# Condition mixing and a quantised gated FFN on one core: new head, scale folded into the down weight, other order of the loop

## The chip, the cores and the metric

The kernel runs on one NeuronCore of a Trainium2 chip. Its engines are TensorE (PE in the profile, PEld for its weight loads), VectorE (DVE), ScalarE (ACT), GpSimd (POOL) and SyncE (SP, which only issues DMAs here). The metric is the device time of one execution in microseconds (us).

## The reference

`x` is (64, 32, 512) in f32: 64 batches of 32 channels by 512. Each batch is mixed over its channels with one of 16 matrices of 32x32, picked by an integer token, and each of the 2048 rows of the result then goes through a quantised gated FFN (512 to 256 to 512). The FFN's result is added to `x`.

```
y = einsum('bct,bcd->bdt', x, weights[token]).reshape(-1, 512).astype(bf16)
for m in (gate, up):                      # dynamic quantisation of each row
    xs = y * inv[m];  scale = max(max|xs| / 127, 1e-8);  q = clip(round(xs / scale), -127, 127)
    h[m] = (q @ w[m].T) * scale * s[m]    # w holds whole numbers up to 127
inter = clip(silu(h[gate]) * h[up], -10, 10).astype(bf16)
xm = inter * inv_inter;  scale_m = max(max|xm| / 127, 1e-8);  qm = clip(round(xm / scale_m), -127, 127)
out = x + (qm @ w_down.T) * scale_m * s_down
```

## The kernel before, in words

The 2048 rows are 16 tiles of 128 rows (four batches each), all of `x` stays in SBUF (`x_sb`). Every engine has its own instruction queue, written out by hand; queues meet only through counting semaphores, and each engine executes its queue in the order written. For a tile t the steps are, with engine and line:

- `mix_in_batch` (TensorE, L560): one f32 product of the block-diagonal 128x128 `mix_all[:, t]` with the 128x512 tile into `y_ps`.
- `y_out` (ScalarE, L255): `y_ps` to bf16 `y_bf`. `smooth` (GpSimd, L206): `xs` = `y_bf` times both smoothing vectors, 128x1024.
- `amax_in`, `scale_in` (VectorE, L359, L364, L367): row maxima of `xs`, the scale, its reciprocal.
- `quantise` (ScalarE, L262): two activations of 128x512 that scale and round (a large bias leaves the whole number in the low f16 bits). `transpose_q` (TensorE, L566): eight 128x128 transposes to `qt_ps`. `q_out` (ScalarE, L269): to bf16 `q_t`.
- `gate_up` (TensorE, L582): eight products, 256 columns each, to `gu_ps`. `gate_up_out` (VectorE, L373): times the weight scales, to `gu`. `gate_silu` (ScalarE, L274). `intermediate` (VectorE, L378), `clip` (VectorE, L385).
- `smooth_mid` (GpSimd, L215), `amax_mid` and `scale_mid` (VectorE, L390, L395, L398), `quantise_mid` (ScalarE, L281), `transpose_mid` (TensorE, L597), `qm_out` (ScalarE, L288).
- `down` (TensorE, L610): two products of 512 columns into `o_ps`. `down_out` (VectorE, L406): times row scale and `s_down`, to `ffn`. `residual` (GpSimd, L222): plus `x`, to `res`, which SyncE stores.

The stages of different tiles are interleaved: in turn i of the loops ScalarE does `qm_out(i-6)`, `quantise(i-2)`, `quantise_mid(i-5)`, `gate_silu(i-3)`, `y_out(i)`, `q_out(i-2)`, and TensorE `gate_up(i-3)`, `mix_in_batch(i)`, `transpose_q(i-2)`, `down(i-6)`, `transpose_mid(i-5)`.

In the head the weights are loaded as they are and transposed by TensorE (`weight`, L532), the vectors are loaded as broadcasts to 128 partitions, and `mix_all` is filled from two sources: for tiles 0 to 2 by one small DMA per batch, whose address comes from a token that `value_load` (L141, L245) reads into a register from `token_row` in SBUF; for tiles 3 to 15 at once, from rows that an indirect DMA gathered (`picked`), which go out to DRAM (`picked_dram`, L166) and come back as four strided DMAs (L173, semaphore `blocks_in`). The program tests a flag at its end, and would repeat all tiles with split weights if the weights were not exact in bf16; with these inputs it does not.

## Time and profile before

| | |
|---|---|
| three runs | 96.28, 96.28, 98.17 us (median 96.28) |
| span of the profiled execution | 96.0 us; its own total was not recorded, the median run is 0.3 us above the span |
| busy | PE 57.0 us (59%), PEld 36.1 (38%), DVE 72.1 (75%), ACT 62.9 (66%), POOL 67.5 (70%) |
| DMA | 12.05 MB, mean 126 GB/s |
| TensorE's granted clock | near full, but about half from 20 to 23.5 us and from about 86 us on |

Busy shares are means over three stages: a head until the first SiLU at 22.9 us, a loop of equal periods, and a tail from about 83 us, in which no new tiles enter.

### The profile page before, as it was taken

What the parts mean: (1) busy time and instruction counts of PE and PEld (TensorE: products, weight loads), DVE (VectorE), ACT (ScalarE), POOL (GpSimd) and SP (SyncE); (2) the same over time, 40 slices, a digit from 0 to 9 for tenths busy, and PEclk for the clock granted to TensorE, in tenths of its full rate; (3) what the DMA queues carried; (4) which work ended last, traced back from release to release, by engine and by line L of the source; (5) the groups of instructions that cost most, each with busy time, mean ns of one, the idle gap of its engine ahead of it and who ended that gap; (6) DMA issues with size and microseconds to landing.
All of it is one profiled execution on the core that took longest, in us unless ns stands there. A gap on an engine that the chain in (4) does not pass through costs nothing.

```text
span 96.0 us, 1583 instructions
## 1 busy us (share of the span) xinstructions
PE 57.0 (59%) x425; PEld 36.1 (38%) x430; DVE 72.1 (75%) x174; ACT 62.9 (66%) x113; POOL 67.5 (70%) x57
## 2 busy tenths in 40 slices
PE   0692737189559487595865958569594574305610
PEld 0691214164426344363443635436352353102100
DVE  5300059407798989999999999999999999996360
ACT  5000226813978999889898898988989878223100
POOL 5505094800858759999999999999999746925720
PEclk9999999966999999999999999999999999965555
DMA  1989639989412312063360633202202022020443
GB/s 33 230 291 376 180 106 272 251 153 321 136 43 73 111 22 92 38 181 117 112 219 6 213 111 111 109 7 109 91 18 109 3 109 106 7 109 0 180 149 114
DMA packets 8796, 12.05 MB, mean 126 GB/s; under 512 B 3026, under 2 KB 3922, under 8 KB 8786
## 3 DMA queue, kind: packets, MB, share of 16 engines
q1 hardware_dynamic: 7906, 10.08, 33.0%
q0 software_dynamic: 400, 1.31, 3.8%
q10 hardware_dynamic: 480, 0.54, 2.7%
q8 instruction: 4, 0.07, 0.3%
q14 instruction: 6, 0.05, 0.2%
HBM read 7.47 MB, written 4.46 MB: 124 GB/s over the span
## 4 chain that ended last, share of the span: by engine, by line
DVE 54%; issue 13%; DMA 11%; PE 11%; ACT 4%; POOL 2%; SPq 1%; POOLq 0%; ACTq 0%
DVE y_ps L359 13%; DVE ffn L406 12%; DVE gu L373 10%; DVE gu_ps L378 7%; DMA raw<-in_L_ffn_w_down 6%; PE gu_ps L582 5%; DMA picked<-in_L_cond_weights,tokens 5%; DVE amax_m L390 4%; PE o_ps L610 3%; ACT q_t L269 3%; DVE rscale L367 2%; PE y_ps L560 2%; POOL raw L195 1%; DVE rest L414 1%; DVE rest_sums L418 1%
## 5 line engine op out<-in xcount | busy, mean ns | idle before, releaser
L206 POOL TENSOR_TENSOR xs<-y_bf,inv_in 128x1024 f32<-128x1024 bf16 x15 | 32.1, 2142 | 10.2 <-ACT y_bf L255 9.6
L582 PE MATMUL gu_ps<-w_t,q_t 128*128 128x256 bf16 x128 | 17.6, 283 | 17.4 <-ACT q_t L269 17.4
L262 ACT ACTIVATE q<-xs,rscale 128x512 f32<-128x512 f32 x32 | 21.4, 724 | 2.1 <-DVE rscale L367 2.1
L222 POOL TENSOR_TENSOR res<-ffn,x_sb 128x512 f32<-128x512 f32 x15 | 19.1, 1271 | 2.7 <-DVE ffn L406 2.7
L359 DVE TENSOR_REDUCE y_ps<-xs 128x2 f32<-128x1024 f32 x16 | 19.5, 1217 | 1.1 <-POOL xs L204 1.1
L560 PE MATMUL y_ps<-x_sb,mix_all 128*128 128x512 f32 x32 | 17.3, 625 | 4.7 <-DMA mix_all<-in_L_cond_weights 2.5
L582 PEld LDWEIGHTS gu_ps<-w_t,q_t 128*128 128x128 bf16 x128 | 11.7, 101 | 21.4 <-ACT q_t L269 20.0
L269 ACT ACTIVATE q_t<-qt_ps 128x1024 bf16<-128x1024 f16 x16 | 16.2, 1014 | 0.3 <-PE qt_ps L566 0.3
L255 ACT ACTIVATE y_bf<-y_ps 128x512 bf16<-128x512 f32 x16 | 9.3, 581 | 10.1 <-PE y_ps L560 10.1
L373 DVE TENSOR_TENSOR gu<-gu_ps,s_in 128x512 f32<-128x512 f32 x16 | 10.9, 683 | 5.5 <-PE gu_ps L582 5.5
L215 POOL TENSOR_TENSOR xm<-clipped,inv_mid 128x256 f32<-128x256 bf16 x16 | 11.7, 732 | 3.6 <-DVE clipped L385 3.6
L406 DVE SCALAR_TENSOR_TENSOR ffn<-o_ps,scale_m,s_out 128x512 f32<-128x512 f32 x16 | 11.9, 743 | 2.8 <-PE o_ps L610 2.8
L274 ACT ACTIVATE gu_ps<-gu,scale 128x256 f32<-128x256 f32 x16 | 7.6, 478 | 9.5 <-DVE gu L373 9.5
L566 PEld LDWEIGHTS qt_ps<-ident_f,q 128*128 128x128 f16 x128 | 8.3, 98 | 9.7 <-ACT q L262 6.2
L610 PE MATMUL o_ps<-w_t,qm_t 128*128 128x512 bf16 x27 | 9.7, 430 | 3.3 <-DVE ffn L406 3.1
L566 PE MATMUL qt_ps<-ident_f,q 128*128 128x128 f16 x128 | 9.8, 219 | 1.1 <-ACT q L262 1.0
L288 ACT ACTIVATE qm_t<-qmt_ps 128x256 bf16<-128x256 f16 x16 | 6.1, 382 | 4.7 <-PE qmt_ps L597 4.7
L281 ACT ACTIVATE qm<-xm,rscale_m 128x256 f32<-128x256 f32 x16 | 8.1, 506 | 0.0
L378 DVE SCALAR_TENSOR_TENSOR gu_ps<-gu,scale,gu_ps 128x256 f32<-128x256 f32 x16 | 7.5, 470 | 0.0
L560 PEld LDWEIGHTS y_ps<-x_sb,mix_all 128*128 128x128 f32 x32 | 5.1, 199 | 6.0 <-issue 5.8
L385 DVE TENSOR_SCALAR clipped<-gu_ps 128x256 bf16<-128x256 f32 x16 | 6.8, 424 | 0.5
L353 DVE TENSOR_TENSOR xs<-y_bf,inv_in 128x512 f32<-128x512 bf16 x1 | 0.7, 693 | 8.6 <-ACT y_bf L255 8.6
(40 smaller groups left out, 54.1 us busy)
## 6 DMA issues: line engine op xcount, KB each, us to landing
x_sb<-in_x SPq DMA_DIRECT2D x16, 256.0 KB, 3.5
out<-res SPq DMA_DIRECT2D x16, 256.0 KB, 2.0
raw<-in_L_ffn_w_gate POOLq DMA_DIRECT2D x1, 512.0 KB
raw<-in_L_ffn_w_up POOLq DMA_DIRECT2D x1, 512.0 KB, 7.6
raw<-in_L_ffn_w_down SPq DMA_DIRECT2D x1, 512.0 KB, 5.6
inv_in<-in_L_ffn_inv_gate ACTq DMA_DIRECT2D x1, 256.0 KB, 4.2
inv_in<-in_L_ffn_inv_up ACTq DMA_DIRECT2D x1, 256.0 KB, 5.5
picked_dram<-picked SPq DMA_DIRECT2D x1, 256.0 KB, 3.2
```

The source lines that it names most:

```text
L206: nc.gpsimd.tensor_tensor(xs[t % 2][:, :, :], y_bf[t % 2][:, :].unsqueeze(1).to_broadcast([P, 2, T]), inv_in[:, :, :], ALU.mult).then_inc( ...
L222: nc.gpsimd.tensor_tensor(res[t % RES][:, :], ffn[t % 2][:, :], x_sb[:, t * T:(t + 1) * T], ALU.add).then_inc(res_done, 1)
L262: nc.scalar.activation(q[t % 2][:, m, :], xs[t % 2][:, m, :], ACT.Copy, bias=ROUND_TO_F16, scale=rscale[:, t, m:m + 1]).then_inc(q_done, 1)
L269: nc.scalar.activation(q_t[t % 2][:, :, :, :], qt_ps[t % 2][:, :, :, :], ACT.Copy, bias=-float(OFFSET)).then_inc(qt_out, 1)
L359: nc.vector.tensor_reduce(y_ps[t % 2][:, 0:2], xs[t % 2][:, :, :], AX.X, ALU.max, apply_absolute_value=True).then_inc(amax_done, 1)
L373: nc.vector.tensor_tensor(gu[t % 2][:, :, :], gu_ps[t % 2][:, :, :], s_in[:, :, :], ALU.mult).then_inc(gu_out, 1)
L378: nc.vector.scalar_tensor_tensor(gu_ps[t % 2][:, 1, :], gu[t % 2][:, 1, :], scale[:, t, 1:2], gu_ps[t % 2][:, 0, :], ALU.mult, ALU.mult).t ...
L406: nc.vector.scalar_tensor_tensor(ffn[t % 2][:, :], o_ps[:, :], scale_m[:, t:t + 1], s_out[:, :], ALU.mult, ALU.mult).then_inc(ffn_done, 1)
L560: nc.tensor.matmul(y_ps[t % 2][:, :], mix_all[:, t, :], x_sb[:, t * T:(t + 1) * T], start=True, stop=True).then_inc(y_done, 1)
L566: last = nc.tensor.transpose(qt_ps[p][:, m, c, :], f16_low(q[p][:, m, c * P:(c + 1) * P]), ident_f16[:, :])
L582: last = nc.tensor.matmul(gu_ps[p][:, m, :], q_t[p][:, m, c, :], w_t[j][:, m, c * I:(c + 1) * I], start=(j == 0 and c == 0), stop=(j == pa ...
L610: last = nc.tensor.matmul(o_ps[:, :], qm_t[p][:, c, :], w_t[j][:, 2, c * T:(c + 1) * T], start=(j == 0 and c == 0), stop=(j == parts - 1 a ...
```

## The change

The arithmetic of the result stays. The host hands the weights over already transposed in chunks, and all vectors as one row, which TensorE spreads over the partitions with a column of ones (`widen`); VectorE and ScalarE copy them out of PSUM. `value_load` now reads the tokens straight from the input in DRAM, and several stand together ahead of their DMAs. `s_down` is multiplied into `w_down` once (`fold_s_down`), which makes it inexact in bf16, so it is split in three bf16 parts (`next_part`) and `down` has six products in place of two. `down_out` adds `x` itself and writes `res`; `residual` is gone. `clip` moves to GpSimd. The scale of the middle of tile t is computed together with that of the input of tile t+3, in one column block of `scale` (`MID_LAG`). Tiles' buffers become three or four deep, the first and last tile go in halves, and the order in all loops is new. The gate and up weights are read in place, every second bf16 of the f32 words.

```diff
-    WARM_UP = 52
+    WARM_UP = 36
+    XS, YB, QB, GB, MB = 4, 3, 3, 3, 3
+    MID_LAG = 3
...
+            sp.dma_start(rows[:, :], vectors.unsqueeze(0)).then_inc(rows_in, 16)
             load(0)
-            load(1)
-            sp.wait_ge(row_in, 16)
-            sp.wait_ge(mix_zero, 1)
-            for t in range(2):
-                for j in range(PER // 2):
-                    early_block(t, j)
-            load(2)
-            for j in range(PER):
-                early_block(2, j)
+            for t in range(EARLY):
+                s = [sp.value_load(token.unsqueeze(0)[0:1, t * PER + j:t * PER + j + 1], min_val=0, max_val=S - 1)
+                     for j in range(PER if t == 2 else PER // 2)]
+                if t == 0:
+                    sp.wait_ge(mix_zero, 1)
+                for j in range(len(s)):
+                    early_block(t, j, s[j])
+                if t + 1 < EARLY:
+                    load(t + 1)
+            sp.dma_start(flat(raw_down), w_down).then_inc(w_down_in, 16)
+            load(3)
             sp.wait_ge(picked_in, 16)
-            load(3)
-            sp.dma_start(raw[0][:, 2, :].rearrange("p (b k) -> p b k", k=I),
-                         w_down.rearrange("(b p) k -> p b k", p=P)).then_inc(w_in[2], 16)
+            load(4)
...
+            def clip(t):
+                pool.wait_ge(inter_done, t + 1)
+                nc.gpsimd.tensor_scalar(clipped[t % MB][:, :], inter[t % MB][:, :], LIMIT, -LIMIT,
+                                        ALU.min, ALU.max).then_inc(clip_done, 1)
...
-            for i in range(TILES + 7):
-                if exists(i - 4):
-                    smooth_mid(i - 4)
-                if exists(i - 7) and i - 7 < TILES - 1:
-                    residual(i - 7)
-                if exists(i):
-                    smooth(i)
+            for t in range(4):
+                smooth(t)
+            for i in range(TILES):
+                clip(i)
+                smooth_mid(i)
+                if exists(i + 4):
+                    smooth(i + 4)
...
             for t in range(2):
-                for j in range(PER // 2, PER):
-                    early_block(t, j)
-            for i in range(TILES + 6):
-                if exists(i - 6):
-                    qm_out(i - 6)
+                s = [act.value_load(token.unsqueeze(0)[0:1, t * PER + j:t * PER + j + 1], min_val=0, max_val=S - 1)
+                     for j in range(PER // 2, PER)]
+                if t == 0:
+                    act.wait_ge(mix_zero, 1)
+                for j in range(PER // 2):
+                    early_block(t, PER // 2 + j, s[j])
...
+            y_out(0)
+            s_in_copy()
+            y_out(1)
+            y_out(2)
+            quantise(0)
+            y_out(3)
+            q_out(0)
+            quantise(1)
+            y_out(4)
+            for i in range(TILES + 2):
+                if exists(i):
+                    gate_silu(i)
                 if exists(i - 2):
-                    quantise(i - 2)
-                if exists(i - 5):
-                    quantise_mid(i - 5)
-                if exists(i - 3):
-                    gate_silu(i - 3)
-                if exists(i):
-                    y_out(i)
-                if exists(i - 2):
-                    q_out(i - 2)
+                    qm_out(i - 2)
+                if exists(i + 1):
+                    q_out(i + 1)
+                if exists(i + 2):
+                    quantise(i + 2)
+                if exists(i - 1):
+                    quantise_mid(i - 1)
+                if exists(i + 5):
+                    y_out(i + 5)
...
-            def scale_in(t):
-                dve.wait_ge(amax_done, t + 1)
-                nc.vector.tensor_scalar(scale[:, t, :], y_ps[t % 2][:, 0:2], 1.0 / QMAX, LEAST_SCALE,
+            def scale_columns(t, m, end):
+
+                if m < 2:
+                    dve.wait_ge(amax_done, halves_through(t) - (1 if split(t) and end == 1 else 0))
+                if end == 3:
+                    dve.wait_ge(amaxm_done, t - MID_LAG + 1)
+                nc.vector.tensor_scalar(scale[:, t, m:end], amax[:, t, m:end], 1.0 / QMAX, LEAST_SCALE,
                                         ALU.mult, ALU.max).then_inc(scale_done, 1)
-                dve.wait_ge(scale_done, t + 1)
-                nc.vector.reciprocal(rscale[:, t, :], scale[:, t, :]).then_inc(rscale_done, 1)
+                dve.wait_ge(scale_done, scales_through(t, end - 1))
+                nc.vector.reciprocal(rscale[:, t, m:end], scale[:, t, m:end]).then_inc(rscale_done, 1)
...
             def down_out(t):
                 dve.wait_ge(down_done, t + 1)
-                nc.vector.scalar_tensor_tensor(ffn[t % 2][:, :], o_ps[:, :], scale_m[:, t:t + 1], s_out[:, :],
-                                               ALU.mult, ALU.mult).then_inc(ffn_done, 1)
-
+                if t >= RES:
+                    dve.wait_ge(stored[t % RES], 16 * (t // RES))
+                nc.vector.scalar_tensor_tensor(res[t % RES][:, :], o_ps[:, :], scale[:, t + MID_LAG, 2:3],
+                                               x_sb[:, t * T:(t + 1) * T], ALU.mult, ALU.add).then_inc(res_done, 1)
...
+            def fold_s_down():
+                dve.wait_ge(w_down_in, 16)
+                dve.wait_ge(s_out_wide, 1)
+                nc.vector.tensor_tensor(w_out[0][:, :, :], raw_down[:, :, :],
+                                        o_ps[:, :].unsqueeze(1).to_broadcast([P, IC, T]), ALU.mult).then_inc(part_done, 1)
+
+            def next_part(j):
+                dve.wait_ge(part_done, j)
+                nc.vector.tensor_tensor(flat(w_out[j]), flat(w_out[j - 1]), bf16_top(flat(w_out[j - 1])),
+                                        ALU.subtract).then_inc(part_done, 1)
...
-            for i in range(2, TILES + 6):
-                if exists(i - 6):
-                    down_out(i - 6)
-                if exists(i - 2):
-                    gate_up_out(i - 2)
+            scales(1)
+            amax_in(2)
+            rest_in_gate_up()
+            fold_s_down()
+            for i in range(TILES + 1):
                 if exists(i):
-                    amax_in(i)
-                if i == 2:
-                    weight_out(2)
-                if exists(i - 3):
-                    amax_mid(i - 3)
+                    gate_up_out(i)
+                if exists(i - 1):
+                    amax_mid(i - 1)
+                if i == LAST - 3:
+                    smooth_gate(LAST)
+                if i == LAST - 2:
+                    amax_half(LAST, 1)
+                scales(i + 2)
                 if exists(i):
-                    scale_in(i)
-                if exists(i - 3):
-                    scale_mid(i - 3)
-                if exists(i - 2):
-                    intermediate(i - 2)
-                    clip(i - 2)
-                if i == TILES:
-                    rest_in_gate_up()
-                if i == TILES + 1:
-                    rest_in_down()
-                if i == TILES + 3:
+                    intermediate(i)
+                if i + 3 < LAST:
+                    amax_in(i + 3)
+                if i + 3 == LAST:
+                    amax_half(LAST, 0)
+                if i == 0:
                     raise_flag()
+                    next_part(1)
+                if i == 1:
+                    next_part(2)
+                if exists(i - 2) and i - 2 < LAST:
+                    down_out(i - 2)
+            for h in range(2):
+                down_out_half(h)
...
-
-            def down_products(p, parts):
-                for j in range(parts):
+                transposes_of_mid(t % MB, t % 2).then_inc(qmt_done, 1)
+
+            def down_products(a, dst, first, end):
+                for j in range(PARTS):
                     for c in range(IC):
-                        last = nc.tensor.matmul(o_ps[:, :], qm_t[p][:, c, :], w_t[j][:, 2, c * T:(c + 1) * T],
-                                                start=(j == 0 and c == 0), stop=(j == parts - 1 and c == IC - 1))
+                        last = nc.tensor.matmul(dst, qm_t[a][:, c, :],
+                                                bf16_top(w_out[j][:, c, first:end]),
+                                                start=(j == 0 and c == 0), stop=(j == PARTS - 1 and c == IC - 1))
...
-            mix_in_batch(0)
-            mix_in_batch(1)
-            weight(0)
-            mix_in_batch(2)
+            pe.wait_ge(ones_done, 1)
+            pe.wait_ge(rows_in, 16)
+            for t in range(4):
+                mix_in_batch(t)
             transpose_q(0)
-            weight(2)
-            for i in range(3, TILES + 6):
-                if exists(i - 3):
-                    gate_up(i - 3)
+            mix_in_batch(4)
+            for i in range(TILES + 2):
+                if exists(i - 2):
+                    transpose_mid(i - 2)
                 if exists(i):
-                    mix_in_batch(i)
+                    gate_up(i)
+                if i == 0:
+                    pe.wait_ge(ones_done, 2)
+                    pe.wait_ge(rest_done, 1)
+                    pe.wait_ge(part_done, 1)
+                    nc.tensor.matmul(flag_ps, ones_col[:, :], rest_sum[:, :], start=True, stop=True).then_inc(rest_total, 1)
+                if exists(i + 1):
+                    transpose_q(i + 1)
                 if exists(i - 2):
-                    transpose_q(i - 2)
-                if exists(i - 6):
-                    down(i - 6)
-                if exists(i - 5):
-                    transpose_mid(i - 5)
-                if i == TILES + 2:
-                    add_rests()
+                    down(i - 2)
+                if exists(i + 5):
+                    mix_in_batch(i + 5)
             pe.wait_ge(flag_done, 1)
             with pe.If(pe.value_load(flag[0:1, 0:1].bitcast(I32)) != 0):
```

**TensorE, one turn of the middle of the loop.** Names: `gu_ps` is written by `gate_up`, `y_ps` by `mix_in_batch`, `qt_ps` by `transpose_q`, `o_ps` by `down`, `qmt_ps` by `transpose_mid`. Before:

```order
L560 MATMUL y_ps<-x_sb,mix_all 128x512 [waits scale_done,x_in12]
L566 MATMUL qt_ps<-ident_f,q 128x128 [waits qt_out,q_done]
L566 MATMUL qt_ps<-ident_f,q 128x128 x7
L610 MATMUL o_ps<-w_t,qm_t 128x512 [waits ffn_done,qmt_out]
L610 MATMUL o_ps<-w_t,qm_t 128x512
L597 MATMUL qmt_ps<-ident_f,qm 128x128 [waits qmt_out,qm_done]
L597 MATMUL qmt_ps<-ident_f,qm 128x128
L582 MATMUL gu_ps<-w_t,q_t 128x256 [waits clip_done,qt_out]
L582 MATMUL gu_ps<-w_t,q_t 128x256 x7
```

Now:

```order
L647 MATMUL qmt_ps<-ident_f,qm 128x128 [waits qmt_out,qm_done]
L647 MATMUL qmt_ps<-ident_f,qm 128x128
L628 MATMUL gu_ps<-raw,q_t 128x256 [waits qt_out,inter_done]
L628 MATMUL gu_ps<-raw,q_t 128x256 x3
L628 MATMUL gu_ps<-raw,q_t 128x256 [waits qt_out]
L628 MATMUL gu_ps<-raw,q_t 128x256 x3
L610 MATMUL qt_ps<-ident_f,q 128x128 [waits q_done,qt_out]
L610 MATMUL qt_ps<-ident_f,q 128x128 x3
L610 MATMUL qt_ps<-ident_f,q 128x128 [waits q_done]
L610 MATMUL qt_ps<-ident_f,q 128x128 x3
L660 MATMUL o_ps<-w_out,qm_t 128x512 [waits res_done,qmt_out]
L660 MATMUL o_ps<-w_out,qm_t 128x512 x5
```

`transpose_mid` stands ahead of `gate_up` in both. Before, the order from one `gate_up` to the next was `mix_in_batch`, `transpose_q`, two products of `down`, `transpose_mid`; now it is `transpose_q`, six products of `down`, `mix_in_batch`, `transpose_mid`.

**ScalarE, one turn of the middle of the loop.** Before, from `qm_out` on:

```order
L288 ACTIVATE qm_t<-qmt_ps 128x256 [waits down_done,qmt_done]
L262 ACTIVATE q<-xs,rscale 128x512 [waits qt_done,rscale_done]
L262 ACTIVATE q<-xs,rscale 128x512
L281 ACTIVATE qm<-xm,rscale_m 128x256 [waits qmt_done,rscalem_done]
L274 ACTIVATE gu_ps<-gu,scale 128x256 [waits gu_out]
L255 ACTIVATE y_bf<-y_ps 128x512 [waits xs_done,y_done]
L269 ACTIVATE q_t<-qt_ps 128x1024 [waits gu_done,qt_done]
```

Now, from `gate_silu` on:

```order
L310 ACTIVATE gu_ps<-gu,scale 128x256 [waits gu_out]
L324 ACTIVATE qm_t<-qmt_ps 128x256 [waits qmt_done]
L305 ACTIVATE q_t<-qt_ps 128x1024 [waits qt_done,gu_done]
L292 ACTIVATE q<-xs,rscale 128x512 [waits qt_done,rscale_done]
L292 ACTIVATE q<-xs,rscale 128x512 [waits rscale_done]
L317 ACTIVATE qm<-xm,rscale 128x256 [waits qmt_done,rscale_done]
L285 ACTIVATE y_bf<-y_ps 128x512 [waits xs_done,y_done]
```

Before, `quantise_mid` (`qm`) was the last instruction ahead of the SiLU, and behind the SiLU stood `y_out` and `q_out`; now `qm` is the sixth instruction of the turn that the SiLU opens, and `q_out` the third.

**SyncE, start of the head.** Before:

```order
L152 DMA token_row<-in_itok_B_15 1x64
L138 DMA x_sb<-in_x 128x512 x2
L141 TENSOR_LOAD token_row [waits mix_zero,row_in]
L141 ISA x2
L142 ISA
L142 DMA mix_all<-in_L_cond_weights 32x32
L141 TENSOR_LOAD token_row
L141 ISA x2
```

Now:

```order
L185 DMA rows<-in_vectors 1x2304
L170 DMA x_sb<-in_x 128x512
L188 TENSOR_LOAD in_token_ptr
L188 TENSOR_LOAD in_token
L188 ISA x2
L188 TENSOR_LOAD in_token_ptr
L188 REGISTER_ALU
L188 TENSOR_LOAD in_token
L188 ISA x2
```

Each value takes two loads now, of the input's address (`in_token_ptr`) and of the token in DRAM, where it took one from SBUF; SyncE does this for eight tokens, all ahead of the DMA to `picked_dram`, and ScalarE for four.

## Rows read from the trace of the kernel before

**Rows 1.** The page's chain that ended last: share of the span by engine.

```profile
DVE 54%; issue 13%; DMA 11%; PE 11%; ACT 4%; POOL 2%; SPq 1%; POOLq 0%; ACTq 0%
```

**Rows 2.** Windows: stretch, length, busy us and instructions per engine, clock, DMA share, GB/s.

```profile
20.00:23.50 3.50, 3.50 (x16) 1.95 (x14) 1.31 (x2) 0.48 (x1) 0.00 (x0) 0.52 0.97 258
...
50.00:54.07 4.07, 2.90 (x23) 1.84 (x22) 3.97 (x11) 3.80 (x8) 4.01 (x5) 1.00 0.39 125
```

**Rows 3.** Timeline of ScalarE, one period: start, length, engine, line, operation.

```profile
52.66 0.38 ACT L288 ACTIVATE qm_t<-qmt_ps 128x256 bf16<-128x256 f16 x1
52.92 1.34 ACT L262 ACTIVATE q<-xs,rscale 128x512 f32<-128x512 f32 x2
54.15 0.51 ACT L281 ACTIVATE qm<-xm,rscale_m 128x256 f32<-128x256 f32 x1
54.93 0.48 ACT L274 ACTIVATE gu_ps<-gu,scale 128x256 f32<-128x256 f32 x1 [0.27 <-DVE gu L373]
55.34 0.58 ACT L255 ACTIVATE y_bf<-y_ps 128x512 bf16<-128x512 f32 x1
55.82 1.01 ACT L269 ACTIVATE q_t<-qt_ps 128x1024 bf16<-128x1024 f16 x1
56.73 0.38 ACT L288 ACTIVATE qm_t<-qmt_ps 128x256 bf16<-128x256 f16 x1
```

**Rows 4.** Timeline of an early period, GATE_UP products and SiLU.

```profile
25.24 1.05 PE L582 MATMUL gu_ps<-w_t,q_t 128*128 128x256 bf16 x8 [1.16 <-ACT q_t L269]
...
27.05 0.48 ACT L274 ACTIVATE gu_ps<-gu,scale 128x256 f32<-128x256 f32 x1 [0.64 <-DVE gu L373]
...
29.02 1.05 PE L582 MATMUL gu_ps<-w_t,q_t 128*128 128x256 bf16 x8 [1.42 <-ACT q_t L269]
```

**Rows 5.** Timeline of TensorE's matmuls, one period.

```profile
53.71 1.02 PE L560 MATMUL y_ps<-x_sb,mix_all 128*128 128x512 f32 x2
54.57 0.61 PE L566 MATMUL qt_ps<-ident_f,q 128*128 128x128 f16 x8
55.02 0.59 PE L610 MATMUL o_ps<-w_t,qm_t 128*128 128x512 bf16 x2
55.45 0.28 PE L597 MATMUL qmt_ps<-ident_f,qm 128*128 128x128 f16 x2
```

**Rows 6.** Waits: who waited for whom, us in total, times, longest.

```profile
ACT qm_t L288 <- PE qmt_ps L597: 4.7, 2, 3.5
```

**Rows 7.** SyncE's register loads of a token from SBUF, ns min/median/max.

```profile
L141 SPq TENSOR_LOAD <-token_row x8: 267/273/471, 2.1 to 10.5; - x8
```

**Rows 8.** VectorE's register load of the flag at the end, ns.

```profile
L506 DVEq TENSOR_LOAD <-flag x1: 833/833/833, 92.5 to 92.5; - x1
```

**Rows 9.** Timeline of SyncE's DMA issues in the head.

```profile
1.17 0.84 SPq L138 DMA_DIRECT2D x_sb<-in_x  x2
3.07 3.64 SPq L142 DMA_DIRECT2D mix_all<-in_L_cond_weights  x4
...
13.99 0.79 SPq L168 DMA_DIRECT2D raw<-in_L_ffn_w_down  x1
16.06 1.90 SPq L173 DMA_DIRECT2D mix_all<-picked_dram  x4
```

**Rows 10.** DMA issues by tensor: KB each, median us to landing.

```profile
picked_dram<-picked SPq DMA_DIRECT2D x1, 256.0 KB, 3.2
...
mix_all<-picked_dram SPq DMA_DIRECT2D x4, 52.0 KB, 3.2
```

**Rows 11.** Groups of instructions: busy us, mean ns, idle before.

```profile
L406 DVE SCALAR_TENSOR_TENSOR ffn<-o_ps,scale_m,s_out 128x512 f32<-128x512 f32 x16 | 11.9, 743 | 2.8 <-PE o_ps L610 2.8
L215 POOL TENSOR_TENSOR xm<-clipped,inv_mid 128x256 f32<-128x256 bf16 x16 | 11.7, 732 | 3.6 <-DVE clipped L385 3.6
...
L385 DVE TENSOR_SCALAR clipped<-gu_ps 128x256 bf16<-128x256 f32 x16 | 6.8, 424 | 0.5
```

**Rows 12.** Timeline of the last computation, VectorE.

```profile
92.47 0.69 DVE L503 TENSOR_TENSOR res<-ffn,x_sb 128x512 f32<-128x512 f32 x1
```

505 lines of the change are left out of this document (260 added, 245 removed).

## The prediction

> **What bounds the kernel now.** I read the chain that ended last first: VectorE has 54% of it, "issue" 13% [rows 1]. That is a mean over stages, so I looked at windows. In one period of 4.07 us in the middle VectorE is busy for 3.97, GpSimd for 4.01 and ScalarE for 3.80, TensorE for 2.90 at full clock [rows 2]: the loop is filled by VectorE and GpSimd together, and ScalarE is close behind. Then I read the timeline of one ScalarE period for what each activation takes when the next follows at once: from start to start SiLU 0.41, `qm_out` 0.26, `q_out` 0.91, the two of `quantise` 1.23, `y_out` 0.48, and `quantise_mid` lasts 0.51 [rows 3]. The reader is to see that only 0.27 us ahead of the SiLU is idle there: ScalarE alone could turn in about 3.7 us.
>
> Early on, while no `down` runs yet, the period is another: from `gate_up` at 25.24 to the next at 29.02, 3.78 us [rows 4]. It is a circle: `gate_up` to SiLU takes 27.05 - 25.24 = 1.81 us (products, then `gate_up_out`) [rows 4], then SiLU 0.41, `y_out` 0.48, `q_out` 1.01, and 0.05 for the semaphore [rows 3], sum 3.76. So a walk along the queues with these lengths gives the period to 0.02 us, and I use the same walk on the new order.
>
> **The change, the loop.** What it takes away is on the two full engines: `clip`, 0.42, and two small operations leave VectorE; `residual` leaves GpSimd, which gets `clip`. That one is not shown there: from below 0.42, VectorE's time for it, from above 0.73, the two-input `smooth_mid` of the same shape [rows 11]. I take 0.7, the row of the same engine. With GpSimd at 4.01 less a residual and plus 0.7, both engines have room for a period of 3.7. Merged scales, deeper buffers and the `x` added in `down_out` (0.74 as before, same shape [rows 11]) I cost at nothing: they lie on VectorE beside ScalarE's longer turn. If GpSimd's room were gone, the clip would cost its length in every turn.
>
> What the change adds is a new circle. Take the start of SiLU(i) as zero. ScalarE then does, in its order, SiLU 0.41, `qm_out` 0.26, `q_out` 0.91, `quantise` 1.23, `quantise_mid(i-1)` 0.51: that one ends at 3.32 [rows 3]. TensorE's next turn opens with `transpose_mid(i-1)`, which waits for it, and `gate_up(i+1)` stands behind that, though its own input was ready at 0.41 + 0.26 + 1.01 = 1.68. With 0.05 for the semaphore, 0.2 for the two transposes until the next product starts (between 0.1, if they only cost their columns, and their 0.28 [rows 5]) and 1.81 to SiLU(i+1), the period is 3.32 + 0.05 + 0.2 + 1.81 = **5.38 us**. Before, `quantise_mid` was the last activation ahead of the SiLU, and `transpose_mid` had no wait to show.
>
> There is a second circle on TensorE: `qm_out(i-2)` ends at 0.41 + 0.38 = 0.79, then come the six products of `down`, 3 times the 0.43 that two take from start to start, then the mix, 0.86 [rows 5]: 0.79 + 0.05 + 1.29 + 0.86 = 2.99. It ends ahead of 3.37, so the six products cost nothing as long as the first circle stands; without the first the period would be 2.99 + 0.2 + 1.81 = 5.0. Queued behind the waiting `transpose_mid` are `gate_up`, and through it `gate_up_out` on VectorE and the SiLU, so all engines idle.
>
> From SiLU(0) to SiLU(15): the first step has no `quantise_mid`, VectorE's turn with the flag and `next_part(1)` is the longest, about 4.0 (estimate from VectorE's operations, `next_part` at 1.2); the second lacks `qm_out`, 5.1; then 12 steps of 5.38 = 64.6; the last has no `quantise` left, 5.38 - 1.23 = 4.2. Sum **77.9**.
>
> **The head.** `mix_in_batch(3)` now stands ahead of `transpose_q(0)`, and it waits for `blocks_in`, the last link of a chain on SyncE. Per token, before: four blocks are issued in 3.64 us; with 0.42 for one issue (a pair of x loads takes 0.84) that is (3.64 - 0.42)/3 = 1.07 from one to the next [rows 9], of it 0.27 for the load from SBUF [rows 7]; 0.38 stays beside the issue. Now a token costs 0.38 + 2 L, L being one load, and eight of them stand in SyncE's queue ahead of `picked_dram`. L from DRAM is not shown: from below 0.27, the load from SBUF [rows 7]; the nearest from above is 0.83, the flag's load that has to wait for its engine [rows 8]; for the far end I go half as far again, 1.3. I take 0.55, the middle of the two rows, so 1.48 per token. SyncE: first two issues until 1.6 (a pair takes 0.84 from 1.17 [rows 9], one of them the new row of vectors), eight tokens 8 x 1.48 = 11.8, eight block DMAs 3.4, x loads 0.42 each for three, `w_down` 0.79 [rows 9]: `picked_dram` starts at 1.6 + 11.8 + 3.4 + 1.3 + 0.8 = 18.9. It lands 3.2 later; the last of four block DMAs starts 1.45 after the first (1.90 for all four [rows 9]) and lands 3.2 later [rows 10]. That is 26.8, and about 1 less since a megabyte of broadcasts is gone from the queues: **25.8**. Before, those four DMAs started at 16.06 [rows 9], now at about 22, so the head is 6 us later there.
>
> The Trainium skill has a floor for such a load (DMA: Bandwidth & Descriptors, "Latency and other measured facts": about 600 ns). By it L would be 0.6 and the sum 0.8 us longer; no row of this trace shows a load from DRAM.
>
> Behind `blocks_in`: TensorE has idled, and the row shows that it then runs at half clock for about 3.5 us (0.52 [rows 2]); mix(3) 1.7, transposes 0.9, mix(4) 1.7, then `gate_up` to SiLU(0) 1.8: **6.1**. The new second table load of ScalarE falls into ScalarE's wait there; if that cover were gone it would add its length, little over 1 us. Weights transposed by the host save TensorE 24 transposes that now lie beside the wait for DMA: nothing.
>
> **The tail.** From SiLU(15): SiLU 0.48 [rows 3], `intermediate`, clip, `smooth_mid` 0.5 + 0.7 + 0.73 [rows 11]. Then `down_out(13)` holds VectorE until about 3.0. `amax_mid` and scales 0.8, `quantise_mid` 0.51; `down(14)` in front until about 4.4; transposes, `qm_out` 0.38; `down` in halves, first 0.8, second 0.65 more, last half of `down_out` 0.45: 7.2. Behind the last computation, ending at 92.47 + 0.69 = 93.16 before [rows 12], come 2.8 us until the span's end. Sum **10.0**, against about 13 before.
>
> **Sum.** 25.8 + 6.1 + 77.9 + 10.0 = 119.8 us of span, against 96.0. The median of the runs is 0.3 above the span, so **120.1 us**, 25% slower.
>
> **Rivals.**
> - *Loads from DRAM cost no more than from SBUF*, L = 0.27 to 0.35, and landings of 2.5 in the lighter queues: `blocks_in` at 21 to 23, total 115 to 117. For it: both are loads into a register of the same sequencer. Against it: a way to DRAM and back. Chance 0.25.
> - *Loads from DRAM cost 1.3 or more*: 8 x 2 x 0.75 = 12 us more, 132. Chance 0.09.
> - *Faster*: the circle does not close, since TensorE takes the ready `gate_up` past the waiting `transpose_mid`. Then ScalarE's 3.7 bounds the loop. SiLU(0) at 32 (27 with cheap loads), 15 x 3.75 = 56, tail 10: 98.6, or 93.6 with cheap loads. It decides when the period is under 3.8 and the loads are cheap. Against it: in the tail ScalarE waited up to 3.5 us for `transpose_mid` [rows 6], whose `qm` was long written, since the queue held `down` in front, waiting for VectorE: matmuls stay in order. Chance 0.05. The same rival is that the change does only what its parts say.
> - *Strided weights at half rate*: `gate_up` and `down` now stream every second bf16. If that halves TensorE's rate, `gate_up` is 0.85 longer and the second circle binds (2.99 + 1.29 + 0.2 + 1.81 + 0.85 = 7.1): 145. No row shows a strided moving operand. Chance 0.03.
> - Between these (period near 5.0 or shorter, head early) 0.08, at 105 to 114.
>
> The forecast has 0.50. The range has to hold 8 in 10: from 111, the cheap loads with a period 0.3 shorter, to 129, loads of 0.83 (8 x 2 x 0.28 = 4.5) with periods 0.15 longer and a tail at half clock. A measurement of this kernel tells about 2% from no change. Faster by over 2%: 0.03; within 2%, 94.4 to 98.2: 0.03; slower by over 2%: 0.94.
>
> **What would show it.** Right: in the middle of the loop a period of 5.3 to 5.5 on all engines; the products of `gate_up` idle ahead, ended by the transposes or by `qm` of ScalarE; VectorE near 65% busy; ScalarE idle ahead of the SiLU for 1.6 us a turn; mix(3) late, at 26, behind blocks from `picked_dram`, with register loads of about 0.55 on SyncE; the first SiLU at 32. Wrong: a period under 4.5, `gate_up` starting 0.05 behind `q_out`, or mix(3) before 22.

## The result, and the profile after

The changed kernel takes **130.64 us** (median of four runs, 128.78 to 131.22); the kernel before, run beside it, 97.22 (median of four, 96.28 to 99.25). The ratio is 1.342, 95% interval 1.326 to 1.358: slower by a third. Some executions run one to five per cent longer than others of the same kernel, so each ratio here compares the faster executions only, and each time is the median of all. The forecast was 120.1, range 111 to 129: right in direction, with the top of the range 1.6 us too low. The profiled execution took 130.45 us, with a span of 128.7.

First the page's busy times and the chain that ended last, which answer [rows 1]:

```profile
PE 80.0 (62%) x463; PEld 43.8 (34%) x470; DVE 69.7 (54%) x140; ACT 66.0 (51%) x118; POOL 53.3 (41%) x55
...
PEclk9995555555589975699999999999999999999999
...
ACT 25%; PE 23%; issue 18%; SPq 15%; DVE 13%; DMA 3%; ACTq 0%; DVEq 0%
```

VectorE had 54% of the chain and now 13%; no engine is full. SyncE's queue, 1% before, has 15%, and it is all in the head. One window over a period, and one over the first turns of the loop (columns as in [rows 2]):

```profile
61.27:66.59 5.32, 3.80 (x25) 2.21 (x26) 3.63 (x8) 3.86 (x7) 3.19 (x3) 1.00 0.28 97
46.00:53.00 7.00, 5.23 (x24) 3.39 (x26) 4.38 (x9) 4.29 (x9) 5.88 (x5) 0.56 0.00 0
```

Every engine idles for at least 1.46 of 5.32 us, where two were full before. ScalarE's timeline shows what it waits for, one period, against [rows 3]:

```profile
61.27 0.48 ACT L310 ACTIVATE gu_ps<-gu,scale 128x256 f32<-128x256 f32 x1 [1.47 <-DVE gu L444]
61.69 0.36 ACT L324 ACTIVATE qm_t<-qmt_ps 128x256 bf16<-128x256 f16 x1
61.95 1.01 ACT L305 ACTIVATE q_t<-qt_ps 128x1024 bf16<-128x1024 f16 x1
62.85 1.33 ACT L292 ACTIVATE q<-xs,rscale 128x512 f32<-128x512 f32 x2
64.08 0.50 ACT L317 ACTIVATE qm<-xm,rscale 128x256 f32<-128x256 f32 x1
64.53 0.60 ACT L285 ACTIVATE y_bf<-y_ps 128x512 bf16<-128x512 f32 x1
66.59 0.48 ACT L310 ACTIVATE gu_ps<-gu,scale 128x256 f32<-128x256 f32 x1 [1.46 <-DVE gu L444]
```

TensorE in the same period, against [rows 5]:

```profile
62.34 1.30 PE L660 MATMUL o_ps<-w_out,qm_t 128*128 128x512 bf16 x5 [1.39 <-ACT qm_t L324]
63.48 1.02 PE L605 MATMUL y_ps<-x_sb,mix_all 128*128 128x512 f32 x2
64.63 0.29 PE L647 MATMUL qmt_ps<-ident_f,qm 128*128 128x128 f16 x2
64.75 1.07 PE L628 MATMUL gu_ps<-raw,q_t 128*128 128x256 bf16 x8
```

`qm` ends at 64.08 + 0.50 = 64.58, the transposes of `qmt_ps` start at 64.63, and `gate_up` follows at 64.75. Its own input `q_t` was there at 61.95 + 1.01 = 62.96. So for 1.8 us `gate_up` is ready and does not start. Most of that it stands behind `down` and the mix, which would let the next product start at 63.48 + 0.86 = 64.34 (the mix takes 0.86 from its start to the next product); the last 0.41 us are the wait of `transpose_mid` for `qm`. That 0.41 is what the first circle costs over the second, and experiment 5 gets it back.

In the head, SyncE's register loads (ns min/median/max), against [rows 7]. One token now needs one of each:

```profile
L188 SPq TENSOR_LOAD <-in_token_ptr x8: 828/842/1957, 1.6 to 19.0; - x8
L188 SPq TENSOR_LOAD <-in_token x8: 459/463/496, 3.3 to 19.9; - x8
```

SyncE's DMA issues from tile 2's blocks on, against [rows 9], and the landings of both transfers, against [rows 10]:

```profile
20.82 1.83 SPq L173 DMA_DIRECT2D mix_all<-in_mix_w  x4
22.69 0.42 SPq L196 DMA_DIRECT2D raw_down<-in_w_down  x1
23.16 0.43 SPq L170 DMA_DIRECT2D x_sb<-in_x  x1
23.64 0.53 SPq L199 DMA_DIRECT2D picked_dram<-picked  x1
24.21 0.56 SPq L170 DMA_DIRECT2D x_sb<-in_x  x1
28.37 2.13 SPq L204 DMA_DIRECT2D mix_all<-picked_dram  x4
```

```profile
picked_dram<-picked SPq DMA_DIRECT2D x1, 256.0 KB, 4.7
...
mix_all<-picked_dram SPq DMA_DIRECT2D x4, 52.0 KB, 2.1
```

What stands behind `blocks_in`: mix(3) on TensorE, then the second table load and SiLU(0) on ScalarE. The table load ends at 39.09 while `gu` was ready at 38.62, so it was not quite covered:

```profile
32.44 2.04 PE L605 MATMUL y_ps<-x_sb,mix_all 128*128 128x512 f32 x2 [6.50 <-issue]
...
37.81 1.28 ACT L310 ACT_TABLE_LOAD   x1
39.11 0.48 ACT L310 ACTIVATE gu_ps<-gu,scale 128x256 f32<-128x256 f32 x1
```

Later SiLUs start at 43.13, 49.23, 55.95 and 61.27, then every 5.32 us until 114.48, and the last at 118.64. The last computation answers [rows 12], and the clip on GpSimd [rows 11]:

```profile
125.94 0.48 DVE L471 SCALAR_TENSOR_TENSOR res<-y_ps,scale,x_sb 128x256 f32<-128x256 f32 x1 [0.20 <-PE y_ps L660]
...
L237 POOL TENSOR_SCALAR clipped<-inter 128x256 bf16<-128x256 bf16 x16 | 6.4, 399 | 38.8 <-DVE inter L451 38.8
```

### The profile page after: what moved, and what is told of

It reads as the page before. It is cut to its first block, busy times and chain, and to the rows that moved or that the text cites. A ratio compares the mean times of both kernels' runs of the same rounds, so it can differ in the third digit from the quotient of the medians.

```text
span 128.7 us, 1643 instructions
## 1 busy us (share of the span) xinstructions
PE 80.0 (62%) x463; PEld 43.8 (34%) x470; DVE 69.7 (54%) x140; ACT 66.0 (51%) x118; POOL 53.3 (41%) x55
## 3 DMA queue, kind: packets, MB, share of 16 engines
q10 hardware_dynamic: 480, 1.07, 2.6%
## 4 chain that ended last, share of the span: by engine, by line
ACT 25%; PE 23%; issue 18%; SPq 15%; DVE 13%; DMA 3%; ACTq 0%; DVEq 0%
ACT q L292 13%; SPq L188 11%; PE gu_ps L628 11%; DVE gu L444 8%; PE o_ps L660 6%; ACT qm_t L324 4%; ACT qm L317 4%; DMA x_sb<-in_x 3%; PE qmt_ps L647 3%; PE y_ps L605 3%; SPq L173 2%; ACT q_t L305 1%; DVE res L463 1%; SPq L170 1%; ACT L310 1%
## 5 line engine op out<-in xcount | busy, mean ns | idle before, releaser
L660 PE MATMUL o_ps<-w_out,qm_t 128*128 128x512 bf16 (+1 forms) x89 | 23.3, 395 | 19.5 <-ACT qm_t L324 17.8
L417 DVE TENSOR_REDUCE amax<-xs 128x2 f32<-128x1024 f32 x14 | 17.0, 1214 | 10.5 <-POOL xs L232 10.5
L237 POOL TENSOR_SCALAR clipped<-inter 128x256 bf16<-128x256 bf16 x16 | 6.4, 399 | 38.8 <-DVE inter L451 38.8
L628 PE MATMUL gu_ps<-raw,q_t 128*128 128x256 bf16 x128 | 17.9, 283 | 1.3 <-ACT q_t L305 1.3
L660 PEld LDWEIGHTS o_ps<-w_out,qm_t 128*128 128x128 bf16 x96 | 8.2, 99 | 29.2 <-ACT qm_t L324 19.7
L463 DVE SCALAR_TENSOR_TENSOR res<-o_ps,scale,x_sb 128x512 f32<-128x512 f32 x15 | 11.3, 750 | 6.8 <-PE o_ps L660 5.9
L605 PEld LDWEIGHTS y_ps<-x_sb,mix_all 128*128 128x128 f32 x32 | 6.8, 237 | 22.9 <-issue 21.5
L628 PEld LDWEIGHTS gu_ps<-raw,q_t 128*128 128x128 bf16 x128 | 11.9, 98 | 5.1 <-issue 3.1
L610 PE MATMUL qt_ps<-ident_f,q 128*128 128x128 f16 x128 | 10.7, 231 | 0.0
L647 PE MATMUL qmt_ps<-ident_f,qm 128*128 128x128 f16 x32 | 4.6, 224 | 7.5 <-ACT qm L317 6.4
L317 ACT ACTIVATE qm<-xm,rscale 128x256 f32<-128x256 f32 x16 | 8.0, 502 | 1.0 <-DVE rscale L429 1.0
L451 DVE SCALAR_TENSOR_TENSOR inter<-gu,scale,gu_ps 128x256 bf16<-128x256 f32 x16 | 7.5, 470 | 0.9 <-ACT gu_ps L310 0.7
```

The lines of the kernel that those rows point to most:

```text
L317: nc.scalar.activation(qm[t % MB][:, :], xm[t % MB][:, :], ACT.Copy, bias=ROUND_TO_F16, scale=rscale[:, t + MID_LAG, 2:3]).then_inc(qm_don ...
L417: nc.vector.tensor_reduce(amax[:, t, 0:2], xs[t % XS][:, :, :], AX.X, ALU.max, apply_absolute_value=True).then_inc(amax_done, 1)
L463: nc.vector.scalar_tensor_tensor(res[t % RES][:, :], o_ps[:, :], scale[:, t + MID_LAG, 2:3], x_sb[:, t * T:(t + 1) * T], ALU.mult, ALU.add ...
L605: nc.tensor.matmul(y_ps[t % 2][:, :], mix_all[:, t, :], x_sb[:, t * T:(t + 1) * T], start=True, stop=True).then_inc(y_done, 1)
L610: last = nc.tensor.transpose(dst[:, c, :], f16_low(q[a][:, m, c * P:(c + 1) * P]), ident_f16[:, :])
L628: last = nc.tensor.matmul(gu_ps[p][:, m, :], q_t[a][:, m, c, :], bf16_top(raw[j][:, m, c * I:(c + 1) * I]), start=(j == 0 and c == 0), sto ...
```

## The experiments

Theory A: two separate causes. Loads from DRAM in SyncE's queue hold the head up, and in the loop a circle through two in-order queues sets the period, no engine's work. The rivals were the six products of `down` (TensorE's work), the two engines VectorE and GpSimd, and TensorE's clock. For the ratios, the kernel before took 97.39 us beside experiments 1, 2, 5 and 6, 97.46 beside 7 to 10, 97.53 beside 4, 11, 12 and 13, and 96.95 beside 3, 14 and 15. Kernel 10 is the kernel of experiment 10, and so on; steps and periods are from one SiLU to the next.

**1. Tokens from SBUF in the changed kernel.**

```diff
+            sp.dma_start(token_row[:, :], token.unsqueeze(0)).then_inc(row_in, 16)
-                s = [sp.value_load(token.unsqueeze(0)[0:1, ...
+                s = [sp.value_load(token_row[0:1, ...
```

ScalarE's four loads are changed in the same way.

> The changed kernel with the tokens loaded once to SBUF (a 64-value row) and read into registers from there, as before the change; all else as in the change. Theory A (the register loads from DRAM hold SyncE back): a token costs about 0.7 us instead of 2.0, eight of them 10 us less, the product of tile 3 starts at about 22 to 23 us instead of 32.4, the loop keeps its period of 5.32, time 118 to 121. Rival B (the head is late by the DMAs' landings and their order, the loads are hidden beside them): less than 4 us gained, time 126 or more.

Measured: 118.67 us, ratio 1.223 (1.198 to 1.247), 12 us less than the changed kernel. SiLU(0) goes from 39.11 to 29.08, the period stays 5.32, and `picked_dram` is issued at 12.86, about where it stood in the kernel before (12.80):

```profile
12.86 0.57 SPq L203 DMA_DIRECT2D picked_dram<-picked  x1
```

So the loads are worth the 10 us before SiLU(0), and the loop does not care. About 2 of the 12 come later: the second and third step from SiLU to SiLU take 5.37 and 5.32 us here at full clock, and 6.10 and 6.72 in the changed kernel, partly at half clock.

**2. The reverse: tokens from DRAM in the kernel before.** The edit is the same in the other direction.

> The kernel before with one part of the change alone: the tokens are read into registers straight from DRAM. Theory A: eight tokens on SyncE cost 1.3 us more each, the product of tile 2 stands ahead of the second weight's transposes and tile 0's, so all behind it comes 9 to 10 us later: time 105 to 107, period 4.07 as before. Rival B: less than 3 us, time under 100.

Measured: 110.37 us, ratio 1.137 (1.116 to 1.159). SiLU(0) goes from 22.9 to 35.8, while the periods stay 4.07. It cost 3 to 5 us more than expected. The tokens' loads are those of the changed kernel, two for each, but both loads of the first token are much longer here, 2.40 and 2.19 us on SyncE (and 1.61 and 2.67 on ScalarE), which is most of the excess; why is open:

```profile
L141 SPq TENSOR_LOAD <-in_itok_B_ptr x8: 822/831/2402, 2.1 to 22.0; - x8
L141 SPq TENSOR_LOAD <-in_itok_B x8: 452/474/2193, 4.6 to 23.0; - x8
```

**3. Half of it: only tile 2's four tokens from SBUF**, the other eight from DRAM.

> The changed kernel with tile 2's four tokens read from SBUF and the other eight (four on SyncE, four on ScalarE) from DRAM as in it. Theory A (one price per token, 1.97 against about 0.65): 4 x 1.3 = 5.3 us off the time at which picked_dram is issued, less 0.4 for the added DMA, and so 4.5 to 5.5 us off the total: 125 to 126. Rival B (the first loads are dear and the later ones would be cheap anyway): 2 us or less. Rival C (the tokens of tiles 0 and 1, on ScalarE as well, hold the head by themselves, so that SyncE's later tokens hide): under 3 us.

Measured: 122.91 and 126.17 us, median 124.5, so 6.1 under the changed kernel; the profiled execution is the longer one. SiLU(0) goes from 39.11 to 33.66. `picked_dram` is issued at 18.31 instead of 23.64, 5.3 earlier for four tokens:

```profile
18.31 0.52 SPq L205 DMA_DIRECT2D picked_dram<-picked  x1
```

1.3 us per token, as theory A has it, net of the 0.4 for the added DMA. With two executions so far apart the total only excludes rivals B and C; the time of the issue is the sharper reading.

**4. The rest of the chain to `blocks_in`.** `picked_dram` ahead of `w_down` and x tile 3 on SyncE, the Silu table loaded at the start of ScalarE.

```diff
+            sp.wait_ge(picked_in, 16)
+            sp.dma_start(picked_dram, picked[:, :]).then_inc(picked_out, 16)
             sp.dma_start(flat(raw_down), w_down).then_inc(w_down_in, 16)
             load(3)
+            act.preload_act_table(ACT.Silu)
```

> The changed kernel, tokens from DRAM as in it, with picked_dram issued ahead of w_down and x tile 3 on SyncE, and the Silu table loaded at the start of ScalarE. Theory A (part of the 4.7 us landing of picked_dram, 3.2 before, is the 0.75 MB queued ahead of it, and the second table load holds SiLU(0) up by 0.4): picked_dram issued 0.9 earlier, landing 3.2, SiLU(0) 0.4 less: 2.5 to 2.8 us under the changed kernel. Rival B (4.7 is the DMA's own time, and the table load is hidden): 0.9 us or less.

Measured: 129.31 us, ratio 1.325 (1.309 to 1.342), 1.3 under the changed kernel and half of what theory A said:

```profile
picked_dram<-picked SPq DMA_DIRECT2D x1, 256.0 KB, 3.1
...
mix_all<-picked_dram SPq DMA_DIRECT2D x4, 52.0 KB, 3.8
```

The landing of `picked_dram` falls to 3.1, as expected, but the four block DMAs now take 3.8 instead of 2.1, probably because the 0.75 MB are still on their way then (no row names it). The wait moved from one link of the chain to the next. mix(3) starts 0.72 earlier and SiLU(0) 0.76: what is won is little more than the earlier issue. The table load is out of the way (SiLU(0) starts 0.04 behind `gu`, 0.48 in the changed kernel), but from mix(3) to `gu` it takes 0.42 longer, since full clock comes at the same time as before, 36.7 against 36.6, and so more of the stretch runs at half clock.

**5. `transpose_mid` behind what is ready.**

```diff
-                if exists(i - 2):
-                    transpose_mid(i - 2)
                 if exists(i):
                     gate_up(i)
                 if exists(i + 1):
                     transpose_q(i + 1)
                 if exists(i - 2):
+                    transpose_mid(i - 2)
                     down(i - 2)
```

> The changed kernel with one move on TensorE: the transposes of the middle stand behind gate_up and the transposes of q of their turn, ahead of down, and no longer ahead of gate_up. Theory A (a circle of SiLU, four activations, quantise_mid, transposes of the middle, gate_up): the circle opens, and the next one binds: SiLU 0.41, qm_out 0.38, 0.05, six products 1.29, mix 0.86, gate_up to SiLU 1.81, a period of 4.8, about 0.5 less in each of 13 turns, time 123 to 125. Rival C (the loop is held by TensorE's own work, or by ScalarE's): the period stays at 5.3, time 130.

Measured: 121.76 us, ratio 1.254 (1.227 to 1.282), 8.9 less. The period is 4.90 while mixes run, 0.42 less, and 4.04 in the last four turns, which have no mix; the expectation had left these out, and so asked for 1 to 3 us too little. TensorE in one period:

```profile
60.70 1.53 PE L660 MATMUL o_ps<-w_out,qm_t 128*128 128x512 bf16 x6 [1.04 <-ACT qm_t L324]
62.07 1.02 PE L605 MATMUL y_ps<-x_sb,mix_all 128*128 128x512 f32 x2
62.93 1.07 PE L628 MATMUL gu_ps<-raw,q_t 128*128 128x256 bf16 x8
```

That is the second circle of the prediction: `qm_out`, six products, mix, `gate_up` without a gap, and TensorE idle 1.04 ahead of `down`. Opening one circle gives only the distance to the next.

**6. Two products of `down` instead of six, in the changed order.** The two smaller parts of `w_out` are left out of the sum.

```diff
-                for j in range(PARTS):
+                for j in range(1):
...
```

> The changed kernel with two products in down instead of six; it leaves out the second and third part of the split down weight, so its output is less exact. Theory A: the products are hidden, since the transposes of the middle wait for ScalarE until 3.37 us behind the SiLU and the products and the mix are over at 3.0: the period stays at 5.3, a little gained in the first turns and the tail, time 127 to 129.5. Rival C (TensorE's added work is the cost): 0.86 less a turn, period 4.5, time 117 to 119.

Measured: 130.96 us (129.72 and 132.19): no gain from two thirds of `down` gone. The period stays 5.32 to 0.01 us, so TensorE's work is not the bound. The profiled execution, the longer one, went to half clock at 100.9 us, and three periods grew to 5.9 to 6.2, 2.4 us in all. That blurs the comparison of totals (127 to 129.5 were expected) but not that of the periods:

```profile
60.00:70.00 10.00, 6.03 (x43) 3.58 (x44) 6.53 (x14) 7.48 (x14) 6.36 (x6) 1.00 0.28 87
98.00:110.00 12.00, 7.22 (x40) 4.29 (x40) 7.05 (x14) 6.48 (x13) 3.27 (x5) 0.62 0.12 46
```

TensorE was granted 2.4 GHz in the first stretch and mostly 1.2 GHz in the second. In the 30 us before the clock fell it was busy for 16.7; in the same 30 us of the changed kernel, which kept 2.4 GHz, for 21.7.

**7. Both single repairs, 1 and 5.**

> The changed kernel with both single repairs at once: tokens read from SBUF, and transpose_mid behind gate_up and transpose_q on TensorE. Theory A (two separate causes, a queue of loads in the head and a circle in the loop, that add): SiLU(0) at 29, as with the tokens alone; periods 4.9 with a mix and 4.04 without, as with the order alone; SiLU(15) about 100 and total 111 to 112. Rival B (one gives back part of the other, through the clock of TensorE or through a shared wait): the two gains of 12.0 and 8.9 us do not add, total 114 or more.

Measured: 109.74 us, ratio 1.129 (1.115 to 1.144). SiLU(0) 29.14, periods 4.90 and 4.04. The gains of 12.0 and 8.9 add up to the 20.9 that is measured, so head and loop are separate. The total is 1.3 under the range expected.

**8. The loop opened wholly** (with tokens from SBUF, and with `down_out` one turn later on VectorE).

```diff
-            for i in range(TILES + 2):
-                if exists(i - 2):
-                    transpose_mid(i - 2)
+            for i in range(TILES + 3):
...
-                    down(i - 2)
+                    transpose_mid(i - 2)
+                if i <= TILES and exists(i - 3):
+                    down(i - 3)
```

> Tokens from SBUF, and the loop's order on TensorE opened wholly: gate_up(i), transpose_q(i+1), transpose_mid(i-2), down(i-3), mix(i+5), so that nothing on TensorE waits for what ScalarE does in the same turn; down_out goes one turn later on VectorE. Theory A (the period was a wait in an in-order queue, no engine's work): the period becomes the longest sum of one engine: TensorE 1.07 + 0.43 + 0.2 + 1.29 + 0.86 = 3.85, ScalarE 3.75, VectorE about 3.6; so 3.8 to 3.9, and the total 29 + 4 + 14 x 3.87 + 10.3 + 1.8 = about 99 to 101. Rival B (clip on GpSimd and the larger VectorE operations lengthen each other once they run side by side all the time, smooth 3.12 for 2.14): period 4.3 or more, total 106 or more.

Measured: 103.01 us, ratio 1.056 (1.037 to 1.076). The period is 3.98: theory A's side, but above its 3.87. The expected total was 99 to 101. The first four steps took 4.0, 4.9, 3.8 and 5.2 us, 2.3 more in all than the expectation had for them.

**9. The head in another order** besides: `picked_dram` ahead of tile 2's tokens, the weights' DMAs ahead of the copies, mix(3) behind `transpose_q(0)`, VectorE's weight work in turns 0 and 2, and smaller moves that the expectation lists.

> As the one before, and the head in another order: picked_dram is issued ahead of the third tile's tokens, weights ahead of inv_gate_copy, Silu table loaded at the start, mix(0) and mix(1) ahead of the widening of s_in and s_down, mix(3) behind transpose_q(0) and mix(4) behind gate_up(0), the pass over the low bits of the weights behind intermediate(0), the parts of w_out in turn 2. Theory A (what is left over before is the head's order, 29.1 against 22.9 to the first SiLU): SiLU(0) at 21 to 23, the loop 2 us longer for VectorE's extra work in turns 0 to 2, total 93 to 96, that is, just under before. Rival B (the head's length is TensorE at half clock whatever the order): SiLU(0) at 26 or later, total 98 or more.

Measured: 101.46 us, ratio 1.051 (1.035 to 1.067). SiLU(0) came at 24.4, between the two theories, and the total is on the side of rival B, for a reason that neither had: the third SiLU-to-SiLU step took 8.2 us. The two `next_part` passes together took 4.30 us beside GpSimd's `smooth`, against 2 x 1.28 in the changed kernel; `gate_up_out(3)` stood behind them on VectorE, and `down(0)` waited for them on TensorE (3.96 us). The head's gain was given back there.

**10. Four products of `down`** (third part of `w_out` left out).

> As the one before, with four products of down instead of six (the third part of w_out is left out, so s_down times w_down keeps 16 bits of its mantissa). Theory A (with the circle open, TensorE's own sum of 3.85 bounds the loop, and the six products count now, where in the changed kernel they were free): period 3.75, ScalarE's sum, and one pass of VectorE less in turn 2; 2 to 3.5 us under the one before. Rival B (another engine bounds the period already): no more than 1.3 us under it.

Measured: 97.54 us, ratio 1.004 (0.999 to 1.009). 3.9 us less, more than rival B allowed, but the period is still 3.97, so TensorE did not bound it; what was saved is the one pass in turn 2 (the third and fourth step took 5.1 and 4.4 us instead of 8.2 and 5.1). VectorE's timeline of one period shows the bound, and the last row is the GpSimd operation that runs beside:

```profile
57.59 0.68 DVE L451 TENSOR_TENSOR gu<-gu_ps,s_in 128x512 f32<-128x512 f32 x1
58.18 0.41 DVE L463 TENSOR_REDUCE amax<-xm 128x1 f32<-128x256 f32 x1
58.70 0.56 DVE L433 TENSOR_SCALAR scale<-amax 128x3 f32<-128x3 f32 x1
59.30 0.18 DVE L436 RECIPROCAL rscale<-scale 128x3 f32<-128x3 f32 x1
59.39 0.47 DVE L458 SCALAR_TENSOR_TENSOR inter<-gu,scale,gu_ps 128x256 bf16<-128x256 f32 x1
59.77 1.21 DVE L424 TENSOR_REDUCE amax<-xs 128x2 f32<-128x1024 f32 x1
60.90 0.74 DVE L470 SCALAR_TENSOR_TENSOR res<-o_ps,scale,x_sb 128x512 f32<-128x512 f32 x1
61.56 0.68 DVE L451 TENSOR_TENSOR gu<-gu_ps,s_in 128x512 f32<-128x512 f32 x1
...
57.09 2.14 POOL L236 TENSOR_TENSOR xs<-y_bf,inv_in 128x1024 f32<-128x1024 bf16 x1
```

Hardly a gap on VectorE, and 0.56 us for a scale of three numbers per row. It ends at 59.26, `smooth` at 57.09 + 2.14 = 59.23.

**11. `intermediate(i)` ahead of `scales(i+2)`** on VectorE, nothing else.

> The version with four products, with one edit: on VectorE intermediate(i) stands ahead of scales(i+2). Theory A (its period of 3.97 is VectorE's: from start to start 0.59 + 0.52 + 0.60 + 0.09 + 0.38 + 1.13 + 0.66 = 3.97, and the 0.60 is the merged scale of 128x3, which ends only when GpSimd's smooth ends, while the same operation takes 0.17 where GpSimd is idle): the scale falls behind the end of smooth, takes 0.17, and the period goes to ScalarE's 3.67 to 3.70; 10 steps of 0.28 less, total about 94.5. Rival B (ScalarE and its semaphores give 3.97, and the coincidence with smooth is chance): no change, total 97 to 98. Rival C (the scale comes too late for quantise, which then waits): period above 3.97.

Measured: 96.82 us (94.88 to 99.33). The period falls to 3.69, and the scale to 0.16:

```profile
59.86 0.48 DVE L458 SCALAR_TENSOR_TENSOR inter<-gu,scale,gu_ps 128x256 bf16<-128x256 f32 x1 [0.23 <-ACT gu_ps L314]
60.26 0.16 DVE L433 TENSOR_SCALAR scale<-amax 128x3 f32<-128x3 f32 x1
```

Theory A's step is shown in the period, 0.28 us each. The total is less clear: the median moved by 0.7 only, and the lowest execution, 94.88, is near the 94.5 expected. The profiled execution is the longest of the four, and its last SiLU starts at 84.67, where kernel 10 had 84.78. What the periods won it had lost by then in the head (0.7) and in the first turns, above all in turn 2, which took 6.0 us at full clock: there `next_part` started at 36.24, just behind a `smooth` (36.07), and took 3.05 us, against 1.22 in kernel 10, where it started just ahead of `smooth`. Behind the last SiLU it needed 12.8 us, with half clock from 88.1 on; kernel 10 needed 10.7.

**12. The clip back on VectorE**, in kernel 11.

> As e9_scales_behind, with the clip back on VectorE behind intermediate (0.42 by the row of before). Theory A (with the circle open the parts that relieve VectorE count): VectorE's sum 3.6 + 0.35 to 0.42 becomes the bound, period 3.95 to 4.05, total 3 to 4 us above e9. Rival B (VectorE has room beside ScalarE's 3.7, so that the clip on GpSimd bought nothing): within 1 us of e9.

Measured: 97.97 us, ratio 1.014 (1.007 to 1.020); period 3.93 against 3.69. From SBUF in bf16 the clip takes 0.23 us on VectorE, not 0.42, and adds just that. So moving it is worth 0.24 us a turn, about 3 us by the periods, once the loop is open. The medians differ by 1.2 only, near rival B; against the lowest execution of kernel 11 it is 3. In the changed kernel VectorE waited 1.4 us a turn, so there it was worth nothing as far as the rows tell; no run moved it alone there.

**13. The head once more**, on kernel 11: `quantise(0)` and `q_out(0)` ahead of `y_out(2)`, `transpose_q(0)` ahead of mix(2), `fold_s_down` and `next_part(1)` into the head.

> As the one before, with the head once more: quantise(0) and q_out(0) ahead of y_out(2) on ScalarE, transpose_q(0) ahead of mix(2) on TensorE, fold_s_down and next_part(1) ahead of amax_in(2) on VectorE. Theory A: SiLU(0) 1.4 us earlier (24.9 to 23.5), and turn 2 without next_part 1.2 us shorter; total 2.0 to 2.8 us under the one before. Rival B (TensorE at half clock through mix(2) and mix(3) sets gate_up(0) whatever stands ahead): SiLU(0) unmoved, 1.2 us in all.

Measured: 94.37 us (92.33 to 95.37), 2.5 under kernel 11. Turn 2 takes 3.67 us instead of 6.0. SiLU(0) did not move (25.44 against 25.64, where 23.5 was expected), so the mechanism is rival B's. The gain is twice its 1.2 us, because the pass that leaves turn 2 had taken 3.05 there beside `smooth`; without it the turn is 2.4 shorter.

**14. `amax_in(2)` behind `gate_up_out(0)`**, on kernel 13.

> As e10_head_again (four products), with amax_in(2) behind gate_up_out(0) on VectorE, where it held gate_up_out(0) up by 2.1 us while it waited for GpSimd. Theory A (the head is a set of in-order waits like the loop): SiLU(0) 1.5 to 2 us earlier, total 92 to 93.5, about 4% under the kernel before. Rival B (the gain is given back in turn 0, where quantise(2) waits for the late scale): within 0.5 us of e10, 94.

Measured: 93.83 us, ratio 0.970 (0.964 to 0.976), the lowest median of all. Against kernel 13 the 0.5 us cannot be told from none; SiLU(0) came at 24.82, 0.6 earlier and not 1.5 to 2, with TensorE at half clock from 10.2 to 23.9 us. The first step then took 3.99 us instead of 3.50. So what the head won is given back in turn 0: rival B stands.

**15. The same with all six products**, so with every part of the change but the tokens from DRAM, in the new order.

> As e14_amax_behind of the same call, with all three parts of w_out and so six products of down. Theory A (TensorE's sum 1.07 + 0.43 + 0.2 + 1.29 + 0.86 and its semaphores, 3.98 in e7, bounds the loop now): period 3.95 to 4.0 against 3.69, and next_part(2) in the head, in all 4 to 5.5 us above e14, so level with the kernel before. Rival B (3.98 was VectorE's alone, with the scale behind smooth; TensorE can do it in 3.87): period 3.87, 2.5 to 3.5 us above e14.

Measured: 94.56 us, ratio 0.978 (0.973 to 0.983): **faster than the kernel before by 2.2%** (by 1.7 to 2.7), and only 0.7 above kernel 14. The periods alternate between 3.86 and 3.68, mean 3.77, with TensorE busy without a gap:

```profile
59.78:67.32 7.54, 7.54 (x53) 4.51 (x52) 6.95 (x15) 7.49 (x15) 6.39 (x7) 1.00 0.19 73
```

So six products cost 0.08 us a turn here, less than either theory said. The 3.98 that I took for TensorE's sum was VectorE's, as in kernel 10, and even my 3.85 from single operations was 0.08 too long.

## Why the prediction was right in direction and too low

**The loop: right, mechanism and size.** Period 5.32 against 5.38, set by `quantise_mid`, then `transpose_mid`, then `gate_up`. At full clock the whole loop fits too: 77.4 us from SiLU(0) to SiLU(15) in experiment 1, where 77.9 was forecast. The second circle, hidden in the changed kernel, is there (4.90 in experiment 5 against 5.0 less the 0.2 for the transposes), and the six products cost nothing behind the first (experiment 6). VectorE was said to be near 65% busy: 3.63 of 5.32 is 68%. One reading was off without harm: ScalarE alone takes 4.07 less 0.27, so 3.80 us a turn by [rows 3] and not 3.7; no term of the sum used it.

**The rivals.** That TensorE would pass the waiting transposes is excluded by both timelines. The strided weights are excluded: the eight products of `gate_up` take 1.07 us, 1.05 before. Cheap loads are excluded by the load rows. Nearest to the truth was the rival of dear loads, 132 us, which had a chance of 0.09.

**The step that failed: the price of a load from DRAM**, taken as 0.55 us, the middle between a load from SBUF and the flag's load. Against the profiled 130.45 the terms come out so (us):

| term | forecast | measured | added |
|---|---|---|---|
| `picked_dram` issued | 18.9 | 23.64 | 4.7 |
| from there to the block DMAs | 3.2 | 4.73 | 1.5 |
| block DMAs to mix(3) | 3.7 | 4.07 | 0.4 |
| mix(3) to SiLU(0) | 6.1 | 6.67 | 0.6 |
| SiLU(0) to SiLU(15) | 77.9 | 79.5 | 1.6 |
| tail | 10.0 | 10.06 | 0.1 |
| span to time | 0.3 | 1.75 | 1.4 |

The sum of the last column is 10.3, all of the difference. Without the DMA issues between them, the eight tokens took 16.5 us (1.54 to 5.96, 7.48 to 11.46 and 12.75 to 20.82), 2.06 each instead of 1.48. I gave both loads of a token one price, and the rows show two: 0.46 for the token, which lies even below my 0.55, and 0.83 to 1.96 for the address, at or above my upper row of 0.83. The address load is 0.83 to 0.85 for five of the eight, and 1.65, 1.24 and 1.96 for the first one of each tile. So eight tokens are 9.0 for the addresses, 3.7 for the tokens and 3.8 for the register operations around them (0.47 each, where I had 0.38). The Trainium skill's floor of about 600 ns (DMA: Bandwidth & Descriptors, "Latency and other measured facts") does not hold here for the token's load, 0.46; the address's, at least 0.83, lies above it. With 0.83 for each load, the row that I had called the nearest from above, the forecast would have been 124.6, still 6 us short. Experiments 1, 2 and 3 show the size from both sides.

**The smaller terms.** The landing of `picked_dram` was 4.7, not 3.2: the 0.75 MB ahead of it share the queues, and experiment 4 shows that moving them only shifts the wait. I had subtracted 1 us for lighter queues instead. The first turns of the loop ran partly at 1.2 GHz (0.56 of the full clock from 46 to 53 us), which is more than the 1.6 us of the loop's row: experiment 1 ran them at full clock and was 2.1 shorter there. TensorE had regained 2.4 GHz at 36.6, before SiLU(0), and lost it again at 46.8, behind 3.4 us without a product (43.1 to 46.55); experiment 1 had the same wait and kept the clock, so the cause is open. Third, I set the profiled span of 96.0 beside the median of other runs. All executions that have both show 1.7 to 1.95 us between span and time (96.73 and 94.9 in one of the kernel before), so the gap of 0.3 was never one of a single execution. The clip took 0.40 us on GpSimd where 0.7 was put down, which moved no term. The tail's 10.0 is two errors that cancel: 7.8 us from SiLU(15) to the end of the last computation for 7.2, and 2.2 behind it for 2.8.

## What to carry to other kernels

Walk each in-order queue with measured lengths before costing any operation: an instruction that waits for the end of another engine's turn makes everything behind it wait, and the parts that relieve full engines then pay nothing (the same parts, in another order and with the tokens from SBUF, made this kernel 2.2% faster). When the walk gives a circle, look for the second one, which sets what removing the first is worth. A value read from an input in DRAM into a register is two loads here, and the one for the address is mostly the longer (0.83 against 0.46 us): count both, for each value and on each queue.

## What the runs showed of the hardware

- A scale of 128x2 or 128x3 from SBUF to SBUF on VectorE takes 0.17 us, and 0.5 to 1.2 when GpSimd's two-input `smooth` runs: it ends with it. The 128x1 scale in the kernel before took 0.13 in the middle of a `smooth`, and so did the 128x2 from PSUM, 0.15. Merging the two small scales, with the maxima in SBUF now, made one that can be held up. In the changed kernel it happened once, with the pair

```profile
43.53 0.99 DVE L426 TENSOR_SCALAR scale<-amax 128x3 f32<-128x3 f32 x1
...
41.37 3.12 POOL L232 TENSOR_TENSOR xs<-y_bf,inv_in 128x1024 f32<-128x1024 bf16 x1
```

- The scale ends at 44.52, `smooth` at 44.49. This `smooth` itself took 3.12 instead of 2.14: `next_part` (two inputs in SBUF) had started 0.16 ahead of it and ran until 42.49. In experiment 11 it was the other way round, and `next_part` took 3.05. `amax_mid` (0.40, from 43.02) and `gate_up_out`, which reads PSUM (0.68, from 42.42), ran beside the same `smooth` at their usual length. The Trainium skill (SBUF — State Buffer, "SBUF: two separate sides") says that the port pair of the two engines is "an exclusive lock, not a bandwidth split"; both lengths agree with that.
- The clip with one input took 0.40 us on GpSimd, 0.23 on VectorE from SBUF in bf16, and 0.42 there from PSUM in f32.
- The load of an input's address took 0.82 to 0.86 us in 14 of the 24 cases of the changed kernel and experiment 2, and 0.96 to 2.40 in the others. In the changed kernel's SyncE queue the long ones (1.24, 1.65, 1.96) stand behind DMA issues, but that is not the rule: in experiment 2 all eight on SyncE stand right behind a DMA issue, and five of them took 0.82 to 0.84, and on ScalarE of the changed kernel a load behind another token's took 1.31. Why some take longer is open.
- Experiment 6, with two thirds of `down` left out, fell to 1.2 GHz at 100.9 us in its profiled execution, where the changed kernel, with 80.0 us of products, kept 2.4. Its two executions had a mean clock of 0.77 and 0.80, the changed kernel's four 0.87 to 0.93. That fewer products cost the clock is likely, but no other run tests it.
